# Reordering the last block's output products and moving two subtractions from VectorE to GpSimd

## What is computed

```python
act = silu(h1) * h3                       # one per chosen expert, 512 wide
out_e = act @ w2.T + 2 * (act @ a2[e].T) @ b2[e].T
out = w_first * out_first + w_second * out_second      # the two chosen experts of a token
x = x + out
```

## Time and profile before

| what | us |
|---|---|
| median of three runs | 326.31 (326.28 to 327.21) |
| the profiled execution, its own time | 325.95 |
| its span in the profile | 324.2 |
| TensorE busy | 298.4 (92% of the span) |
| VectorE busy | 225.4 (70%) |
| ScalarE busy | 194.2 (60%) |
| GpSimd busy | 181.7 (56%) |
| mean granted TensorE clock | 0.98 of full speed |

### The profile page before, as it was taken

One profiled execution on the slowest core, in us unless ns is written; L12 is line 12 of the kernel. 1 busy time (PEld: TensorE's weight loads), 2 busy tenths in 40 slices (PEclk: granted clock), 3 DMA queues, 4 the chain that ended last, 5 costly groups with the idle time before them and its releaser, 6 DMA issues. The chain is left out here.

```text
span 324.2 us, 4571 instructions
## 1 busy us (share of the span) xinstructions
PE 298.4 (92%) x1535; PEld 241.4 (74%) x1535; DVE 225.4 (70%) x612; ACT 194.2 (60%) x322; POOL 181.7 (56%) x164
## 2 busy tenths in 40 slices
PE   1865689999999999999999999999999999998994
PEld 1644467888888878878787888888787878786873
DVE  2768757797568956696668956696658945972475
ACT  1153666477674786587664776487655757663431
POOL 2111079925795278816795288717781289417920
PEclk9999599999999999999999999999999999999998
DMA  6521002000200002000100011000000000000000
GB/s 187 166 71 64 2 1 65 2 0 1 68 32 0 2 10 88 2 0 3 65 32 3 0 30 70 0 0 2 1 32 2 1 0 32 2 1 3 32 0 32
DMA packets 7271, 8.95 MB, mean 28 GB/s; under 512 B 1232, under 2 KB 3792, under 8 KB 7248
## 3 DMA queue, kind: packets, MB, share of 16 engines
q1 hardware_dynamic: 5664, 7.54, 7.1%
q10 hardware_dynamic: 1584, 1.12, 1.3%
HBM read 6.56 MB, written 2.10 MB: 27 GB/s over the span
## 5 line engine op out<-in xcount | busy, mean ns | idle before, releaser
L738 ACT ACTIVATE silu<-h_ps 128x512 f32<-128x512 f32 x64 | 38.2, 596 | 37.9 <-PE h_ps L507 37.0
L974 DVE TENSOR_TENSOR act_first<-silu,h_ps 128x512 f32<-128x512 f32 x32 | 22.0, 687 | 44.3 <-ACT silu L738 24.4
L507 PE MATMUL h_ps<-um_hi,b_hi 128*128 128x512 f32 x128 | 51.4, 402 | 0.1
L507 PE MATMUL h_ps<-um_hi,b_lo 128*128 128x512 f32 x128 | 50.9, 398 | 0.0
L507 PE MATMUL h_ps<-um_lo,b_hi 128*128 128x512 f32 x128 | 50.8, 397 | 0.0
L1178 POOL TENSOR_TENSOR heads<-e_o,rec_o 128x512 f32<-128x512 f32 x8 | 14.6, 1827 | 61.0 <-DVE rec_o L904 61.0
L1206 POOL TENSOR_TENSOR scaled<-act_second,ratio 128x512 f32<-128x512 f32 x24 | 30.9, 1291 | 21.0 <-DVE act_second L974 20.7
L497 PE MATMUL h_ps<-t_hi,w_hi 128*128 128x512 f32 x64 | 28.7, 448 | 1.9 <-ACT ratio L730 1.9
L1184 POOL TENSOR_TENSOR um_lo<-umf,um_hi 128x1024 fp32r<-128x1024 f32 x8 | 19.1, 2391 | 18.6 <-ACT um_hi L734 18.6
L974 DVE TENSOR_TENSOR act_second<-silu,h_ps 128x512 f32<-128x512 f32 x32 | 21.4, 684 | 10.8 <-PE h_ps L507 10.8
L507 PEld LDWEIGHTS h_ps<-um_lo,b_hi 128*128 128x128 f32 x128 | 24.2, 189 | 5.8
(11 more groups left out here) (196 smaller groups left out, 781.4 us busy)
## 6 DMA issues: line engine op xcount, KB each, us to landing
x_in<-in_x_dram SPq DMA_DIRECT2D x8, 256.0 KB, 3.0
ctx_in<-in_ctx_t_dram SPq DMA_DIRECT2D x7, 256.0 KB, 3.2
out_dram<-y SPq DMA_DIRECT2D x7, 256.0 KB, 2.0
w_raw<-in_w_t_dram SPq DMA_DIRECT2D x2, 256.0 KB, 6.2
b_raw<-in_b_dram ACTq DMA_DIRECT2D x2, 256.0 KB, 4.9
ctx_in<-in_ctx_t_dram ACTq DMA_DIRECT2D x1, 256.0 KB, 3.8
w2a_raw<-in_w_t_dram SPq DMA_DIRECT2D x1, 256.0 KB, 3.6
w2a_raw<-in_a_t_dram SPq DMA_DIRECT2D x1, 256.0 KB, 4.2
```

Of the source, the lines that this page charges most:

```text
L507: mm = nc.tensor.matmul(banks[n % 2][:], b13[w][:, s, cols], um[k][m][:, s, :], start=False, stop=(i == 2), skip_group_check=True)
L738: nc.scalar.activation(silu[:, n % SILU_RING, :], h1_ps[n % 2][:], ACT.Silu).then_inc(silu_done.sem, 1)
L974: nc.vector.tensor_tensor((act_first, act_second)[k][:, c, :], silu[:, n % SILU_RING, :], h3_ps[n % 2][:], ALU.mult).then_inc(act_done.sem, 1)
```

## The change

In the last block alone (`late` is false), all four w2 products of TensorE go behind the a2 products of chunk 3. In the last block alone, VectorE no longer makes `b_low(1)` and `b_low(2)`; GpSimd makes them at the end of its program, behind `scale_step(7, 2)`, with a new semaphore `last_b_lo` for which `a2_product` waits in place of `b_lo_done`. The other seven blocks are as they were.

```diff
+        last_b_lo = sem("last_b_lo")
...
                 if c < 2:
                     pe.wait_ge(lo_pair.sem, lo_pair.of(b))
+                elif b == LAST and k == 1:
+                    pe.wait_ge(last_b_lo, c - 1)
                 else:
                     pe.wait_ge(lo_done.sem, lo_done.of(b, c - 1))
...
-                w2_product(b, 0)
-                w2_product(b, 1)
-                if late:
+                if late:
+                    w2_product(b, 0)
+                    w2_product(b, 1)
                     lora_in(b + 1, 0)
                     lora_in(b + 1, 1)
                 a2_product(b, 2, 1)
...
                 if not late:
-                    w2_product(b, 2)
+                    for c in range(CHUNKS - 1):
+                        w2_product(b, c)
                 w2_product(b, 3)
...
                 total(b, 3)
-                b_low(b, 1)
-                b_low(b, 2)
+                if late:
+                    b_low(b, 1)
+                    b_low(b, 2)
                 z_low(b, 1)
                 z_low(b, 2)
...
+            for part in (1, 2):
+                pool.wait_ge(b_hi_done.sem, b_hi_done.of(LAST, part + 1))
+                nc.gpsimd.tensor_tensor(b_split[1][:, PARTS[part], :], act_second[:, PARTS[part], :],
+                                        as_f32(b_split[0][:, PARTS[part], :]), ALU.subtract).then_inc(last_b_lo, 1)
```

## The result

| | before | changed |
|---|---|---|
| median of eight runs, us | 326.50 (326.27 to 327.21) | 328.93 (327.39 to 330.47) |
| ratio of the times, 95% interval | | 1.0067 (1.0041 to 1.0092) |
| the profiled execution, its own time | 325.95 | 327.39 |
| its span | 324.2 | 325.6 |

The kernel became slower, by 2.4 us at the medians. The forecast was 327.4 in a range of 326.0 to 329.2, with a chance of 0.51 for slower. The median lies in the range, near its upper end, and the eight times of the changed kernel cover 3.1 us where those of before cover 0.9. (More times of the kernel before, taken beside the experiments, cover 2.2 us in 22 and 2.1 in 35, so a range of times is only a hint.) The profiled execution is the fastest of the eight.

What follows compares the result with a forecast made beforehand. The prediction took the end of z_low(1) on VectorE, for which TensorE waits in the last block, to set the end. Turns with GpSimd add 1.05 us, w2 products 0: 326.31 + 1.05 = 327.36, given as 327.4, range 326.0 to 329.2.

Steps and rivals of the forecast that it cites:

- One event sets the end, z_low(1): Last block: the end of z_low(1) on VectorE releases chunk 2's z product; v_parts starts 2.41 us behind that product's start.
- The subtractions are in series with VectorE's, in the order of asking: Last block: GpSimd's two subtractions alternate with VectorE's totals, ending z_low(1) later by 1.05 us.
- the gain from taking them off VectorE: Last block: without two b_low on VectorE, z_low(1) could end 1.03 us earlier if the engines did not disturb each other.
- The order of turns: Last block: VectorE and GpSimd take turns by who asked first, giving +1.05 us; other orders +0.9 to +1.49.
- rival 1: Last block: VectorE and GpSimd overlap, v_parts starts 1.03 us earlier, time 325.3 us; chance 0.12.
- rival 3: Last block: VectorE does both totals first, then turns alternate with GpSimd; +0.3 us, 326.6 us; chance 0.17.
- The w2 products cost 0, with 0.19 us to spare: Last block: 24 w2 matmuls, 2.83 us, hide behind the mask, sum and rounding chain before b2.
- The clock stays up in the likeliest case: Last block: TensorE keeps 2.4 GHz through its new idle time, so the likeliest time, 327.4 us, has no clock price.
- the prediction's own sign of it: Last block: a2 matmuls standing 0.43 us apart in the changed profile would show the TensorE clock had fallen.
- a stretch that had 0.82 us busy in two: Earlier sparse TensorE work, cited against a clock fall: it still stood at 1.00; the fall came only in the next.
- rival 2: Last block: TensorE's clock falls to 1.2 GHz in its idle time, up to 1.8 us more, 329.2 us; chance 0.18.
- the main case: Last block: GpSimd's subtractions and VectorE's work run in turns, +0.9 to +1.5 us, 327.2 to 327.8; chance 0.48.

Runs made afterwards that it cites:

- the move alone: Only the two w2 products moved behind the a2 products, against the kernel before, both subtractions staying on VectorE: 326.38 us, ratio 1.0008.
- the second profile: The changed kernel run again without any edit; its profiled execution took 328.35 us, median 328.97 us of seven, ratio 1.0066.
- the subtractions alone: The changed kernel with the w2 products back where they stood before, only the two subtractions on GpSimd: 327.90 us, ratio 1.0034.
- the kernel with the fills: The changed kernel plus 12 unused TensorE matmuls, 3 ahead of chunk 2's b product and 9 behind it: 327.41 us, ratio 1.0025.

## Why the prediction was right, and where it was not

- *One event sets the end, z_low(1).* Right: in every profile with the clock at 1.00 and the old order of a2 products, v_parts started 2.34 to 2.41 us behind chunk 2's first z matmul (317.70 - 315.30 = 2.40 in the changed kernel).
- *The subtractions are in series with VectorE's, in the order of asking: +1.05.* Right: +0.97. The two totals ended within 0.01 us of the working, and the gain from taking them off VectorE, forecast at -1.03, is -1.02 where they are left out. The order of turns, which the prediction called not proved, is in the trace.
- *The engines overlap* (rival 1). This did not happen: 3.44 us for two totals. They overlap only where GpSimd fills and does not read.
- *Turns fall well* (rival 3). Not seen in any of four profiles with the subtractions on GpSimd.
- *The w2 products cost 0, with 0.19 us to spare.* Right: b2 at 2.83 behind v_parts, and the move alone makes no difference.
- *The clock stays up in the likeliest case.* This step failed, and the prediction's own sign of it, a2 matmuls 0.43 apart, is in the second profile. I had the price (up to 1.8 us, half of it if the clock rose midway; measured 1.41) and the place (TensorE's idle time ahead of chunk 2's z product), and gave it 0.18. One of two profiles shows it, and 12 of the 15 times of the changed kernel lie at 328.3 or above, where turns alone would put the medians at 326.50 + 0.97 = 327.5 and 326.79 + 0.97 = 327.8, and where only one of ten times of the subtractions alone lies. That most of the other executions fall too is inferred from these times and from the kernel with the fills; one trace shows it directly. I had leaned on a stretch that had 0.82 us busy in two and still stood at 1.00, but the fall came right behind it. What the rows said was that a fall can follow sparse work, and the new gap has only three matmuls in 3.5 us: the clock fell in it in one of the two profiles. Why in one and not in the other stays open.
- *The forecast time.* That the first profiled execution took 327.39 is luck: for an execution like the profiled one the prediction had 327.00, and the rest of the difference is the 0.44 us from the start of the kernel. The median is the other case, 326.50 + 0.97 + 1.41 = 328.9, and it lies in the range because the range took in rival 2 with its full price.
- *Two slips of the working.* z_low(1) is the sixth instruction behind step 7 and not the seventh, and all four orders that the main case lists lie in +0.9 to +1.5; rival 3 is a fifth. Neither changes the sum.

## What to carry to other kernels

Work moved from VectorE to GpSimd is not hidden behind VectorE instructions that read two operands from SBUF, if GpSimd reads SBUF too: add up both durations, in turns, at GpSimd's own length. A wait that opens on TensorE can have a second price, the clock (1.4 us here), which can be missing from the one profile that is looked at: compare the profiled execution with the median first. Where a product waits for an operand, look first for another product that is ready.

## What the runs showed of the hardware that was not expected

- The turns between VectorE and GpSimd are regular: in four profiles the pair of totals took 3.44 to 3.48 us and the pair of subtractions 3.41 to 3.45.
- A fill of 128x1024 by GpSimd takes 0.93 us (1.85 for two), and lets VectorE's instructions with two SBUF inputs run beside it.
- Adding 12 matmuls of no use took 1.6 us off a kernel. In the profile the nine matmuls that mattered ran at 2.4 GHz; without the fills six of them, and part of a seventh, ran at 1.2 GHz in one profile of two.
